# Moving a chunk's softmax division and its rounding residue from VectorE to GpSimd in the loop bodies of an attention-and-feed-forward kernel

## The reference, cut to what matters

```
x = x + 0.5 * ffn(layernorm(x))     # dense 512x512 with bias, plus 8 low-rank experts of rank 16, top 2 by a router
x = x + attention(layernorm(x))     # 32 query heads on 8 key/value heads of 16 features; weights are signs with scales
x = x + 0.5 * ffn(layernorm(x))     # the same feed-forward weights again

# inside attention, for each head:
attn = softmax(q @ k.T / sqrt(16));  out = attn @ v
y = out @ sign(o_weight).T * scale;  y = nan_to_num(y, nan=0, posinf=1e6, neginf=-1e6)
```

## Time and profile before

| what | value |
|---|---|
| median of 3 runs | 1164.65 us (1163.46 to 1167.42) |
| the profiled execution | 1162.77 us |
| its span, first to last instruction | 1161.0 us |
| TensorE busy | 1061.4 us (91%) |
| VectorE busy | 837.9 us (72%) |
| ScalarE busy | 727.0 us (63%) |
| GpSimd busy | 295.4 us (25%) |
| mean granted TensorE clock | 0.959 of full speed |

### The profile page before, as it was taken

The page is one execution under the profiler, slowest core; times in us unless marked ns, Lnnn a source line. Parts: engine busy times, 40 slices in busy tenths (PEclk is TensorE's granted clock), DMA queues, the critical chain, the costliest instruction groups (busy, mean ns, idle before and its releaser), DMA issues.

```text
span 1161.0 us, 16018 instructions
## 1 busy us (share of the span) xinstructions
PE 1061.4 (91%) x5776; PEld 466.8 (40%) x5776; DVE 837.9 (72%) x1107; ACT 727.0 (63%) x1361; POOL 295.4 (25%) x485
## 2 busy tenths in 40 slices
PE   5989887999999999999999999999999999999647
PEld 4778661344334422333334333433343334233236
DVE  5766679767777777876787778777877887871274
ACT  6556432757865786675676667666767675768311
POOL 5355546302420240410050023003200420041010
PEclk9989886999999999999999999999999999999869
DMA  7122331021211123111211121121113010301300
GB/s 254 46 81 88 100 103 49 27 73 36 60 49 35 33 59 105 31 32 48 87 31 31 61 75 31 31 87 48 31 31 110 30 40 17 115 10 33 108 0 37
DMA packets 70507, 68.31 MB, mean 59 GB/s; under 512 B 15132, under 2 KB 52508, under 8 KB 70428
## 3 DMA queue, kind: packets, MB, share of 16 engines
q1 hardware_dynamic: 70428, 67.29, 18.9%
HBM read 41.95 MB, written 24.63 MB: 57 GB/s over the span
## 4 chain that ended last, share of the span: by engine, by line
PE 72%; DVE 13%; ACT 5%; DMA 3%; issue 3%; POOL 3%; SPq 1%; DVEq 0%; ACTq 0%; POOLq 0%
PE ps_out L1516 19%; PE ps_score L1504 18%; PE ps_max L1485 16%; PE ps_fill L1441 5%; DVE neg_max L1312 5%; ACT probs L1018 2%; PE ps_fill L1470 2%; PE ps_fill L1423 2%; PE ps_fill L1445 1%; DVE neg_max L1110 1%; DVE zd L1184 1%; PE ps_out L1441 1%; PE ps_fill L1409 1%; PE ps_fill L1415 1%; DVE xn L1252 1%
## 5 line engine op out<-in xcount | busy, mean ns | idle before, releaser
L1018 ACT ACTIVATE probs<-ps_score 128x512 f32<-128x512 f32 x992 | 539.0, 597 | 262.0 <-PE ps_score L1504 260.9
L1312 DVE TENSOR_REDUCE neg_max<-ps_max 128x1 f32<-128x1024 f32 x480 | 570.9, 1219 | 179.7 <-PE ps_max L1485 177.7
L1504 PE MATMUL ps_score<-qst,kst 99*128 99x512 bf16 x992 | 308.9, 387 | 10.1 <-ACT probs L1018 8.5
L1485 PE MATMUL ps_max<-kst,qst 96*128 96x512 bf16 x1024 | 290.1, 389 | 16.8 <-DVE neg_max L1110 5.8
L1516 PE MATMUL ps_out<-probs,v_ring 128*32 128x512 f32 x2048 | 274.7, 608 | 7.3 <-ACT o_sb L1027 4.9
L1504 PEld LDWEIGHTS ps_score<-qst,kst 99*128 99x128 bf16 x992 | 76.0, 97 | 273.6 <-ACT probs L1018 232.4
L1485 PEld LDWEIGHTS ps_max<-kst,qst 96*128 96x128 bf16 x1024 | 91.4, 99 | 144.5 <-issue 19.5
L852 POOL CAST shift<-neg_max 128x16 bf16<-128x16 f32 x32 | 9.2, 286 | 435.0 <-DVE neg_max L1312 430.6
L1516 PEld LDWEIGHTS ps_out<-probs,v_ring 128*32 128x32 f32 x2048 | 40.9, 108 | 95.6 <-issue 87.2
L948 ACT ACTIVATE xn<-xc,ln_shift,rstd 128x512 f32<-128x512 f32 x48 | 38.6, 814 | 30.6 <-POOL ln_shift L748 19.6
L1441 PE MATMUL ps_fill<-wb_h,xt_h 128*128 128x512 f32 x84 | 47.1, 561 | 1.0 <-DVE xc L1299 0.8
(11 more groups left out here) (254 smaller groups left out, 1296.6 us busy)
## 6 DMA issues: line engine op xcount, KB each, us to landing
qst<-q_dram SPq DMA_DIRECT2D x192, 64.0 KB, 2.2
att_dram<-o_sb SPq DMA_DIRECT2D x31, 256.0 KB, 2.1
q_dram<-zm SPq DMA_DIRECT2D x24, 256.0 KB, 2.6
kst<-k_dram SPq DMA_DIRECT2D x192, 32.0 KB, 2.2
xc<-x SPq DMA_DIRECT2D x8, 512.0 KB, 4.0
x_dram<-xc SPq DMA_DIRECT2D x8, 512.0 KB, 2.9
xc<-x_dram SPq DMA_DIRECT2D x8, 512.0 KB, 5.6
out<-xc SPq DMA_DIRECT2D x8, 512.0 KB, 3.1
```

Of the source, the lines that this page charges most:

```text
L1018: act.activation(probs[:, kt % 2, j, :], score_bank(i, uu, j), ACT.Exp, scale=1.0 / HD ** 0.5).then_inc(probs_ready, 1)
L1312: dve.tensor_reduce(neg_max[:, uu % 2, t:t + 1], ps_max[max_slot(uu, pos)][:, :, :], AXY, ALU.max, negate=True).then_inc(max_read, 1)
L1485: last = pe.matmul(ps_max[slot][:, half, :], qst[0:SR, r, j, q * P:(q + 1) * P], kst[0:SR, r, half * 512:half * 512 + 512], start=True, st ...
L1504: pe.matmul(score_bank(i, uu, j), kst[0:SR + PARTS, uu, kt * P:(kt + 1) * P], qst[0:SR + PARTS, uu, j, :], start=True, stop=True).then_inc ...
```

## The change

In bodies 2 to 7 GpSimd runs the two products of `N0a` and `N0b` and the two subtractions of `N0al` and `N0bl`; VectorE runs them for the two tail chunks only. In `BACK` the order of the four steps becomes `N0a`, `N0b`, `N0al`, `N0bl`, one entry each. That puts `N0a` at entry 14 where it was 15, and `N0b` at entry 15 where it was 16; `N0al` and `N0bl` keep entries 16 and 17. ScalarE's copies L953 move with their names, and so does the tail's order.

```
 BACK:
-    8 * [""] + ["NR", "NL", "", "", "", "", "", "N0a", "N0al N0b", "N0bl", "", "Oa0", ...
+    8 * [""] + ["NR", "NL", "", "", "", "", "N0a", "N0b", "N0al", "N0bl", "", "Oa0", ...

 GpSimd, fill():
+                if pos in ("N0a", "N0b") and not ch.tail:
+                    t = "ab".index(pos[2])
+                    tok = slice(t * P, (t + 1) * P)
+                    gp.wait_ge(att_loaded[ch.att], (ch.att_use + 1) * 16 * DC)
+                    gp.wait_ge(recip_loaded[ch.att], (ch.att_use + 1) * 16 * DC)
+                    gp.tensor_tensor(att_t[ch.att][:, :, tok], att_t[ch.att][:, :, tok], recip_t[ch.att][:, :, tok],
+                                     ALU.mult).then_inc(att_normed[s], 1)
+                if pos in ("N0al", "N0bl") and not ch.tail:
+                    t = "ab".index(pos[2])
+                    tok = slice(t * P, (t + 1) * P)
+                    gp.wait_ge(xt_h_ready[s], ch.t0 + (t + 1))
+                    gp.tensor_tensor(xt_l[s][:, :, tok], att_t[ch.att][:, :, tok], xt_h[s][:, :, tok].bitcast(F32),
+                                     ALU.subtract).then_inc(att_low_ready[s], 1)

 VectorE, fill():
-                if pos in ("N0a", "N0b"):
+                if pos in ("N0a", "N0b") and ch.tail:
...
-                    if ch.tail and t == 0:
+                    if t == 0:
...
-                if pos in ("N0al", "N0bl"):
+                if pos in ("N0al", "N0bl") and ch.tail:
```

More of the change, by code:

```diff
@@ L50 @@
 BACK = [s.split() for s in (
-    8 * [""] + ["NR", "NL", "", "", "", "", "", "N0a", "N0al N0b", "N0bl", "", "Oa0", "Oa1", "C0", "Ob0", "Ob1", "", "G0 C1", "P0", "", "G1", "P1",
+    8 * [""] + ["NR", "NL", "", "", "", "", "N0a", "N0b", "N0al", "N0bl", "", "Oa0", "Oa1", "C0", "Ob0", "Ob1", "", "G0 C1", "P0", "", "G1", "P1",
     "ADD", "", "LN1a", "LN1b", "", "LN1c", "LN1d", "T1a", "T1al", "", "T1b", "T1bl", "", "RT", "", "RU",
```

## The result

| | before | changed |
|---|---|---|
| median | 1164.06 us (4 runs, 1160.85 to 1167.42) | 1180.51 us (4 runs, 1178.71 to 1181.63) |
| ratio, 95% interval | | 1.014 (1.0108 to 1.0171) |
| span of the profiled execution | 1161.0 us | 1179.8 us |
| mean granted clock | 0.959 | 0.951 |

The account below looks back on a forecast made before the run. The prediction took TensorE to bound a body, with ScalarE's order critical. Lateness 14.7, less 1.5 given back, plus 4.5 for the clock, less 0.9 in the tail, made 16.8 us: 1181 us, range 1172 to 1188.

Parts of the forecast that it names:

- ScalarE's order is the path, and it passes the lateness on: Bodies 2 to 7: exponentials 8.2 and 8.3 stand behind both products' copies, late by 14.7 us in all, which reaches TensorE.
- GpSimd's product at 1.28 us: Each product on GpSimd takes 1.28 us, with 0.08 between two instructions; bounds 0.68 and 1.8.
- The second product behind `split_shift`: GpSimd's queue: `N0b` waits for `split_shift` (1.06 us), so exponentials are 1.9 us late in each of bodies 4 to 6.
- Rival (b): Faster: idle GpSimd has the product ready before ScalarE comes, and TensorE's waits in slot 8 vanish: 1153 us; chance 3%.
- its two conditions: What rival (b) needs: the load landing much earlier, or `split_shift` not in the second product's way on GpSimd.
- Given back and clock: Bodies 2 to 7: 0.25 us back in each, 1.5 in all; clock falls cost 4 x 1.1 = 4.5 us.
- When the clock falls: TensorE idle for 2.4 us or more in slots 8 and 9 of bodies 4 to 7; a fall in all six bodies.
- The cast at 0.20 us: First cast of `split_shift` on GpSimd takes 0.20 us in bodies; at 0.59, 0.4 more a body, 2.3 in all.
- The tail: In the tail VectorE does both products before both subtractions, covering ScalarE's copy: a gain of 0.9 us.
- VectorE's relief worth nothing: VectorE's freed 2.7 us per body buy nothing, since TensorE's `turn` waits for the late v products.

Follow-up runs that it names:

- experiment 4: The changed kernel, but on GpSimd both products stand ahead of `split_shift`: 1169.59 us, ratio 1.0054 to the kernel before.
- experiment 5: Against the kernel before: GpSimd does all four steps in the bodies at later entries 17 to 20, projection from 21: 1154.05 us, ratio 0.9914.
- experiment 7: The changed kernel without the load of the inverted sums in the six bodies (output not the reference's): 1177.31 us, ratio 1.0113 to the kernel before.
- experiment 8: The changed kernel without the load of the inverted sums in the bodies and with both products ahead of `split_shift`: 1149.57 us, ratio 0.987 to the kernel before.
- experiment 2: The kernel before, with GpSimd doing all four steps at the old entries: 1187.47 us, ratio 1.0212.
- experiment 3: The kernel before, old entries, with only the subtractions of the six bodies on GpSimd and the products on VectorE: 1163.83 us, ratio 1.0006.
- experiment 6: Against the kernel before: VectorE does all four steps at later entries 17 to 20, projection from 21: 1163.84 us, ratio 0.9998.

## Why the prediction was right, point by point

**ScalarE's order is the path, and it passes the lateness on: shown.** Exponentials 8.2 come later after the inversion by 3.5, 1.6, 3.3, 1.7, 1.7 and 2.3 us in bodies 2 to 7, 14.2 us in all, against 14.7 forecast. Bodies 5 and 6, where the load was early, were forecast at 1.9. The sum fitted better than its parts: the load is what scatters. From its issue to the start of the first product it took 7.3 us in body 2 (449.39 to 456.72), 6.4 in body 4 and 5.0 to 5.5 in the other four. I had taken 5.9 and 6.2 in bodies 2 and 3, 5.3 in the rest; body 3 came out 1.5 cheaper than forecast, body 4 1.4 dearer.

**GpSimd's product at 1.28 us: right,** 1.26 measured, with 1.23 to 1.25 from one start to the next in a pair (experiments 4 and 5), so 1.36 from start to start was 0.1 too much.

**The second product behind `split_shift`: shown,** by experiments 4, 7 and 8. Body 4 of the changed kernel is held by the load, which I had counted as on time; experiment 7, without it, shows the pure queue case, and there the exponentials 8.2 start 683.80 - 670.93 = 12.87 us after the inversion, 1.74 later than before. In bodies 5 and 6 of the changed kernel, where the load was early, it is the same 1.7, against 1.9 forecast.

**Rival (b), faster, was rightly refused and its two conditions rightly named.** Granted one at a time they bring 0.3% (load, not clear of the noise) and 0.9% (queue), granted both they bring 2.7%, to 1149.57 us; the rival's figure was 1153. They add up to more than their sum because ScalarE waits for the later of the two products, and takes both copies before exponentials 8.2.

**Given back and clock: 3.0 forecast, 3.4 measured** between exponentials 8.2 and the projection, and that this fits is luck: two terms are off, and nearly cancel. The clock fell in bodies 2 to 5 and 7, not in body 6. Body 6 gives the plain stretch: 3.88 us against 4.37 before, so 0.5 was given back in a body, 2.9 in six and not 1.5. Against body 6 a fall costs 1.1 to 2.0 us, 8.6 in the five bodies; the two falls of the kernel before cost 2.2, so the clock adds 6.4 us here and not 4.5. There is one fall fewer than forecast, but each lasts 6.8 us and not 3.4, in bodies 2 and 3 too, which I had counted as paid. In bodies 3 and 5 the fall reaches past the first projection matmul, for 0.85 us more in both together, which the sum doesn't have.

**When the clock falls: wrong for one body.** I expected TensorE to stand for 2.4 us or more in each of bodies 4 to 7, and a fall there for that reason. In body 5 it stood for less, 1.71 and 0.44 us, and the clock fell; in body 6 for 1.49 and 0.79, together more than in body 5, and it didn't. The idle time doesn't decide it alone. The stretches from inversion to inversion of bodies 4, 5 and 6 grew by 3.9, 3.6 and 1.2 us, where 2.8 was forecast for each.

**The cast at 0.20 us: right;** in body 4 of the new trace (688.25) it takes 0.20, where the earlier trace rows had 0.59, and 0.20 in the other five bodies. **The tail: right,** 1.1 us against 0.9. From the last inversion to the end it is 87.5 to 87.7 us in the three profiles with the old order (before, experiments 2 and 3) and 86.4 to 87.2 in six with the new one; only experiment 4, with its longer slow clock, has 88.5. **VectorE's relief worth nothing: not tested by itself.** Experiment 3, which frees VectorE of the subtractions, shows no change; the 0.6% of the later entries goes with where the product and the turned rows stand in each queue (experiment 6).

## What to carry to other kernels

Before moving work to an idle engine, write down when its result is needed by the engine that comes for it in order, and what stands ahead of it in the new queue: here 1.0 us of small casts ahead of the second product and a load that lands too late cost more than the longer instruction, which costs nothing once both are out of the way (experiment 8). If the consumer is on the path, move its waiting instruction behind the work that TensorE needs first, and then choose the engine; GpSimd at later entries was 0.8 to 0.9% faster than the kernel before, and VectorE there 0 to 0.2%.

## What the runs showed of the hardware that was not expected

VectorE's product took 1.61 us instead of 0.68 when it began 0.2 us after GpSimd's subtraction (1.26 us), both with two inputs in SBUF (experiment 3). This is the other side of the cast that took 0.59 in the earlier trace rows, and 0.93 us is the greatest part of GpSimd's instruction. By the rule of the Trainium skill (SBUF — State Buffer, "SBUF: two separate sides") VectorE would have waited for GpSimd's whole instruction, until 681.91, and then taken 0.68, which ends at 682.59; it ended at 682.46. The trace agrees, within 0.13 us.

The slow clock is not of one length: 3.4 us in body 2 before, after a wait of 2.18 us for exponentials; 6.8 us in body 4 of the changed kernel, with a wait of 3.38 us; 10.2 us in body 4 of experiment 2, with one of 2.83 us. The single wait doesn't tell the length, then. In experiment 7 TensorE waits 2.6 us in each of the six bodies, and the fall lasts 3.4 us in four of them and 6.8 in bodies 4 and 7. Nor does it tell whether the clock falls: body 7 of experiment 4 fell after a wait of 1.37 us, body 6 of the changed kernel stayed at 1.00 after 1.49 and 0.79. TensorE counts as busy for most of a fall (9.46 of 10.20 us), since its matmuls take longer, so the busy share doesn't show the loss; the granted clock does. What sets the length was not tried.
